# Value products of the attention as one job per step instead of pairs, with a new order of work

## The chip, the cores and the metric

The kernel runs on one core of a Trainium2 chip. The metric is the device time of one launch in microseconds. TensorE (PE in the profile) does the matrix products, VectorE (DVE), ScalarE (ACT) and GpSimd (POOL) work on vectors, and SyncE (SP) issues the DMAs. One program sets every engine's order in advance; engines wait for one another by semaphores only.

## The reference

A transformer block with adaptive normalisation, for 16 batch elements of 1024 tokens and 256 features:

```python
mod = (_silu(c) @ wmod).reshape(16, 6, 1, -1)          # sa, ca, ga, sb, cb, gb
h = _layernorm(x) * (1 + ca) + sa
# attention, 16 heads of 16: scores + ALiBi, causal, softmax, @ V
scores = jnp.einsum('bhqd,bhkd->bhqk', Q, K) / math.sqrt(hd) + slopes * rel
attn = jax.nn.softmax(jnp.where(causal, scores, -jnp.inf), axis=-1)
out = jnp.einsum('bhqk,bhkd->bhqd', attn, V)
x = x + ga * (out @ o_w.T + o_b)
h = _layernorm(x) * (1 + cb) + sb
# feed-forward, 704 wide, activations and weights rounded to an FP4 grid by blocks of 16
x = x + gb * fp4_linear(silu(fp4_linear(h, w_gate)) * fp4_linear(h, w_up), w_down)
```

## The kernel before

**Tiling.** A batch element (below: a batch) is 1024 tokens. Its 16 heads are worked in 4 groups of 4. Attention goes over the scores twice. The maxima half (jobs S, 22 per group, matmuls at L826 and L831) computes scores with the queries on partitions, and VectorE reduces them to a maximum per query (L1251, L1253). The maximum, transposed (MT), is moved into the query tile by a DMA (TOP), so that the attention half can subtract it inside the matmul. The attention half (jobs T, matmuls at L783, L779 and L786) computes scores with the keys on partitions, and ScalarE applies exp and writes the probabilities into the arena in SBUF (L1016).

**Steps.** A group's attention half goes in 12 steps, each one tile of 128 keys against one half (512) of the queries, cut to what is causal: widths 512, 384, 256, 128 for the first half, then 512 five times, 384, 256, 128. That is 4608 columns in all. A step of width 512 or 384 has four T jobs, one per head; the narrow ones have two or one. The arena has `P_SLOTS = 3` slots, each for one step of four heads.

**Value products.** For each step and each of the four heads, TensorE multiplies the values (17 columns: 16 and one of ones, which sums the denominators) by the probabilities (L802). Each float32 product stands as two matmul records in the trace, so a step has eight. The four heads write to output partitions 0, 32, 64 and 96 of one bank, and run in the array side by side. One job PV (L790) handles two steps, s - 1 and s, with s odd: it waits for the exps of step s (`pe.wait_ge(a_free, ...)`), goes through both steps, and adds 1 to the semaphore `pv_done` at the end. All products of one half of the queries add up in one bank; the job that starts a half takes the bank, and a copy on ScalarE (CO, L977) empties it and frees it. ScalarE's exp of a step waits on `pv_done` for the job that holds the step three before it, that is for the whole pair in which this older step stands.

**Other work.** Around the attention stand the layer norm and the projections (TR, U, V: L845, L853, L884), splitting of the queries and keys into three bf16 parts on GpSimd (HIGH, REST, MID, SPL) and the DMAs that lay them out (MOVE), normalising (DEN, RD, RDW, RBC, NUM, MUL), the output projection (O, L904), and the feed-forward half with its rounding to the grid (XR, XQ, HR, HQ on VectorE and GpSimd) and its products (XT L914, GA L925, UP L932, HT L940, DN L947). Batches overlap: the maxima of one batch, the attention of that or the one before and the feed-forward half of the earlier one run at the same time.

**Order.** Nothing sets the order at run time. The class `Plan` builds it once: each job has an engine, a cost, a due time and the jobs that it follows. `settle` (L130) takes, again and again, from all ready jobs the one whose start is earliest, and of equals the one with the earliest due time. The table `SHIFT` adds a constant to the due time for each kind of job and engine; it was found by a search. TensorE's jobs write PSUM through rings that hold at most 4 jobs ahead of ScalarE (A: T, GA, HT, XT, U, V, TR) and 3 ahead of VectorE (D: S, MT, UP, DN, O). PV is in no ring. Two lines price the change of mode between PV and other jobs:

```python
if key[0] == "PE" and MODE.get(key[1][0], 1) != mode:
    t += SWITCH          # 0.095, MODE = {"PV": 4}
```

so in mode 1 a PV that is ready is ranked as if it could start 0.095 us later than any other ready job, and right behind a PV another ready PV is ranked 0.095 us ahead of the rest. Each engine then runs its list strictly in order, with a wait in front of each job: what is queued behind a waiting instruction waits too.

Of the kernel before, what the change touches and what calls it, by code (L numbers as in the profile page):

```python
# [56 lines left out]
TURNS = NS // 2  # L57
# [13 lines left out]
def jobs_of(s):  # L71
    return G // together(s)
# [19 lines left out]
class Plan:  # L92
# [8 lines left out]
    SHIFT = {"ACT CO": 32.0, "ACT GA": -46.0, "ACT HT": -5.0, "ACT KROW": 62.0, "ACT LX": 2.0, "ACT T": -104.0,  # L101
             "ACT TR": 15.0, "ACT U": 55.0, "ACT V": -61.0, "ACT WD": 38.0, "ACT WT": 102.0, "ACT XT": 22.0, "DVE BB": 39.0,
             "DVE BO": -44.0, "DVE DN": -40.0, "DVE HQ": 1.0, "DVE HR": 23.0, "DVE LN": 16.0, "DVE LR": -39.0,
             "DVE MT": 66.0, "DVE N1": 30.0, "DVE N2": 18.0, "DVE N3": 14.0, "DVE O": -15.0, "DVE QROW": -16.0,
# [4 lines left out]
             "POOL MID": -4.0, "POOL MUL": 22.0, "POOL OB": 106.0, "POOL RES": 22.0, "POOL REST": -49.0, "POOL SPL": 61.0,  # L109
# [123 lines left out]
def plan():  # L233
# [64 lines left out]
    def attention(b, at):  # L298
        n, last = 0, ("PE", ("T", b - 1, NG - 1, NS - 1, jobs_of(NS - 1) - 1))
        for g in range(NG):  # L300
            for s in range(NS):
                w = span(s)[1]
                heads = together(s)
                for i in range(jobs_of(s)):
# [5 lines left out]
                       then=(("PE", ("PV", old // (NG * NS), old // NS % NG, old % NS | 1)),) if i == 0 else ())  # L310
# [3 lines left out]
                if s % 2:  # L314
                    first = s - 1 in FIRST
# [124 lines left out]
def adaln_block(nc, x, wq, bq, wk, bk, wv, bv, wo, bo, w_gu, w_down, cond, w_mod, out):  # L440
# [6 lines left out]
    with ExitStack() as ctx:  # L447
# [270 lines left out]
        def _(pe):  # L718
# [47 lines left out]
            def run():  # L766
                for e in PLAN.order["PE"]:
# [22 lines left out]
                    elif kind == "PV":  # L790
                        _, _, g, s = e
                        if s - 1 in FIRST:
                            open_banks(e)
                        if g == 0 and s == 1:
                            pe.wait_ge(a_free, in_a["V", b, 1])
# [679 lines left out]
```

## Time and profile before

| | us |
|---|---|
| median of 3 timed runs | 3579.89 (3577.83 to 3582.98) |
| profiled execution | 3574.78 |
| its span, first to last instruction | 3573.0 |
| TensorE busy | 3351.9 (94%), 21944 matmuls |
| VectorE busy | 3075.8 (86%) |
| ScalarE busy | 1932.1 (54%) |
| GpSimd busy | 1276.6 (36%) |
| value products, L802, busy | 572.5 |

Line numbers (L802) are those of the kernel. Busy time is the union of an engine's instructions. Matmuls are pipelined in the array, so their recorded ends overlap the next start; how much time one takes is read from start to start. "idle before" is time in which the engine had nothing running, and it is put down to the releaser that came last. The mean granted clock of TensorE is 0.980 of full speed; it is below full in the first 250 us and at the very end.

### The profile page before, as it was taken

To read this page: it belongs to the slowest core of one execution; us is meant where nothing else is said; L and a number is where in the kernel's file an instruction comes from. 1 tells how busy PE (TensorE), PEld (TensorE's weight loads), DVE (VectorE), ACT (ScalarE), POOL (GpSimd) and SP (SyncE) were. 2 spreads that over 40 slices of the span, in tenths; PEclk is the share of its full clock that TensorE was granted. 3 is DMA by queue.
4 is the path that set the end of the run, shared out by engine and by line. 5 is a ranking of instruction groups with operands and counts; after the bars stand their busy time and mean duration, and the time that the engine had idled before them with its cause. 6 is when DMAs were issued, how large, how long until landed. Compare 5 with 4: busy or idle time off the path is not lost.

```text
span 3573.0 us, 59366 instructions
## 1 busy us (share of the span) xinstructions
PE 3351.9 (94%) x21944; PEld 2028.7 (57%) x21944; DVE 3075.8 (86%) x5906; ACT 1932.1 (54%) x3630; POOL 1276.6 (36%) x918
## 2 busy tenths in 40 slices
PE   6989999999999999999999999999999999999977
PEld 2335655656656565655655556565565656565556
DVE  8988889888898988889888898988889898887866
ACT  2555555555555555555556555555655555555541
POOL 5122414343243433415343332433324243341333
PEclk7899999999999999999999999999999999999998
DMA  5243333424324342342433333342432433233110
GB/s 119 41 91 46 62 62 48 80 40 76 59 41 77 53 72 43 63 75 42 80 47 62 59 52 67 52 77 40 78 61 41 77 51 69 48 62 57 28 29 12
DMA packets 161812, 208.84 MB, mean 58 GB/s; under 512 B 45172, under 2 KB 101060, under 8 KB 161140
## 3 DMA queue, kind: packets, MB, share of 16 engines
q1 hardware_dynamic: 161524, 205.04, 33.5%
q8 instruction: 176, 2.88, 0.4%
q14 instruction: 112, 0.92, 0.1%
HBM read 66.80 MB, written 18.09 MB: 24 GB/s over the span
## 4 chain that ended last, share of the span: by engine, by line
PE 68%; DVE 21%; ACT 5%; issue 2%; SPq 2%; DMA 2%; POOL 0%; POOLq 0%; DVEq 0%; ACTq 0%
PE banks L802 12%; PE banks L826 11%; PE banks L783 9%; PE banks L947 9%; PE banks L932 7%; PE banks L925 6%; PE banks L853 5%; DVE banks L1253 4%; DVE top L1251 4%; ACT arena L1016 3%; PE banks L884 2%; PE banks L940 2%; PE banks L786 1%; DVE stats L1199 1%; SPq L650 1%
## 5 line engine op out<-in xcount | busy, mean ns | idle before, releaser
L1016 ACT ACTIVATE arena<-banks 128x512 f32<-128x512 f32 (+1 forms) x2432 | 1234.2, 589 | 776.4 <-PE banks L802 316.8
L1253 DVE CUSTOM_DVE_ANT_0 banks<-banks,mask 128x640 f32<-128x640 f32 (+3 forms) x1024 | 1031.5, 1043 | 115.3 <-PE banks L826 108.2
L783 PE MATMUL banks<-qa,ka 105*128 105x512 bf16 (+3 forms) x3072 | 791.6, 329 | 71.9 <-ACT arena L1016 55.0
L826 PE MATMUL banks<-ka,qa 102*128 102x512 bf16 (+3 forms) x3072 | 752.3, 333 | 53.1 <-DVE top L1251 22.6
L802 PE MATMUL banks<-arena,va 128*17 128x512 f32 (+3 forms) x6144 | 572.5, 490 | 11.0 <-DVE top L1253 7.2
L783 PEld LDWEIGHTS banks<-qa,ka 105*128 105x128 bf16 x3072 | 278.3, 97 | 411.1 <-ACT arena L1016 208.8
L826 PEld LDWEIGHTS banks<-ka,qa 102*128 102x128 bf16 x3072 | 262.1, 99 | 400.0 <-issue 96.6
L1150 POOL TENSOR_TENSOR hid<-hid,tm 128x704 f32<-128x704 f32 x128 | 215.0, 1680 | 720.8 <-DVE hid L1227 720.8
L1251 DVE TENSOR_REDUCE top<-banks 128x2 f32<-128x768 f32 (+3 forms) x384 | 386.0, 1040 | 32.9 <-PE banks L831 30.1
L947 PE MATMUL banks<-wdT,hqT 128*128 128x256 f32 x1536 | 363.7, 387 | 3.1 <-ACT hqT L1059 3.0
L947 PEld LDWEIGHTS banks<-wdT,hqT 128*128 128x128 f32 x1536 | 290.3, 193 | 64.5 <-issue 17.3
L802 PEld LDWEIGHTS banks<-arena,va 128*17 128x17 f32 x6144 | 141.3, 97 | 305.5 <-issue 204.8
L786 PE MATMUL banks<-maskT,identb 128*128 128x128 bf16 (+1 forms) x1280 | 296.6, 232 | 0.0
L1054 ACT ACTIVATE hid<-banks 128x352 f32<-128x352 f32 x256 | 114.3, 465 | 247.8 <-PE banks L925 247.3
L1150 POOL TENSOR_TENSOR xb<-xb,tm 128x512 f32<-128x512 f32 x64 | 82.4, 1287 | 372.1 <-DVE xb L1227 372.1
L1167 POOL TENSOR_TENSOR xr<-xr,delta 128x256 f32<-128x256 f32 x128 | 102.3, 799 | 291.3 <-DVE delta L1373 290.9
L1365 DVE TENSOR_TENSOR hid<-hid,banks 128x704 f32<-128x704 f32 x128 | 113.1, 884 | 95.3 <-PE banks L932 95.2
L1153 POOL TENSOR_TENSOR hid<-hid,scaleH 128x704 f32<-128x704 f32 x128 | 178.7, 1396 | 10.0
L925 PE MATMUL banks<-wguTh,xqTh 128*128 128x352 f32 x512 | 180.8, 353 | 1.5 <-DVE xqTl L1316 1.5
L1116 POOL TENSOR_SCALAR parts<-xa 128x1024 bf16<-128x1024 f32 x64 | 73.6, 1150 | 290.8 <-ACT xa L1030 142.9
L925 PE MATMUL banks<-wguTl,xqTh 128*128 128x352 f32 x512 | 166.2, 325 | 0.0
L925 PE MATMUL banks<-wguTh,xqTl 128*128 128x352 f32 x512 | 166.2, 325 | 0.0
(163 smaller groups left out, 5687.1 us busy)
## 6 DMA issues: line engine op xcount, KB each, us to landing
qa<-parts SPq DMA_DIRECT2D x384, 128.0 KB
ka<-parts SPq DMA_DIRECT2D x384, 128.0 KB, 6.6
xa<-in_x SPq DMA_DIRECT2D x16, 1024.0 KB, 8.6
xr<-in_x SPq DMA_DIRECT2D x64, 256.0 KB, 2.7
out_x<-xr SPq DMA_DIRECT2D x64, 256.0 KB, 3.9
rsumT<-rsum_dram SPq DMA_DIRECT2D x63, 256.0 KB
onT<-oT SPq DMA_DIRECT2D x252, 64.0 KB, 5.7
ffn_rows<-rows_dram SPq DMA_DIRECT2D x16, 256.0 KB, 3.1
```

Source lines behind the costliest of these rows:

```text
L783: mm = pe.matmul(ps[:, m * w:(m + 1) * w], ks[0:KT, h, kt * P:(kt + 1) * P], qs[0:KT, h, q0:q0 + w], start=heads < G and m == 0, stop=head ...
L786: mm = pe.matmul(ps[:, 0:heads * w].rearrange("p (h q) -> p h q", h=heads)[:, :, 0:P], identb[:, :], maskT[:, :].unsqueeze(1).broadcast_to ...
L802: mm = pe.matmul(out[32 * h:32 * h + VW, :], va[:, kt, g * G + h, :], probs[:, step % P_SLOTS, h, 0:w], start=step in FIRST, stop=step in ...
L826: mm = pe.matmul(ps[:, at:at + z - a], qs[0:KS, h0 + m, qt * P:(qt + 1) * P], ks[0:KS, h0 + m, a:z], start=qt > 0 and m % paired == 0, sto ...
L925: mm = pe.matmul(ps[:, 0:FH], x, w[:, e[3] * FH:(e[3] + 1) * FH], start=(n == 0), stop=(n == len(terms) - 1))
L932: mm = pe.matmul(ps[:, k * BANK:k * BANK + FH], x, w[:, FF + k * FH:FF + (k + 1) * FH], start=(n == 0), stop=(n == len(terms) - 1))
L947: mm = pe.matmul(ps[:, 0:D], hqT[t % 2][:, c, :], wdT[:, c, :], start=(c == 0), stop=(c == FC - 1))
L1016: nc.scalar.activation(probs[:, s % P_SLOTS, j * heads:(j + 1) * heads, 0:w], ps[:, 0:heads * w].rearrange("p (h q) -> p h q", h=heads), A ...
L1150: nc.gpsimd.tensor_tensor(u, u, m, ALU.subtract).then_inc(gridded, 1)
L1153: nc.gpsimd.tensor_tensor(blocks, blocks, sc.unsqueeze(2).broadcast_to((P, w // BLOCK, BLOCK)), ALU.mult).then_inc(quant_done, 1)
L1251: nc.vector.tensor_reduce(tops, ps, AX.X, ALU.max).then_inc(d_free, 1)
L1253: nc.vector.tensor_tensor_reduce(out=ps, in0=ps, in1=mask[:, S - w:S], scale=1.0, scalar=MASKED, op0=ALU.add, op1=ALU.max, accum_out=tops) ...
```

## The change

One job PV now handles one step. There are 12 per group in place of 6, each waits for its own step's exps alone, and adds 1 to `pv_done`, whose counts at the waiting places are adapted. The exp that reuses a slot waits for one older step, no longer for a pair. The bank of a half is opened by the half's first step. The planner sees PV as single jobs of 1.69 ns per column + 0.02 us, each after the one before it. Where its order puts two or three of them next to each other, they form one run. All values of `SHIFT` are new, so every engine's order is another. The products themselves are the same.

```diff
-    SHIFT = {"ACT CO": 32.0, "ACT GA": -46.0, "ACT HT": -5.0, ... "ACT T": -104.0,
+    SHIFT = {"ACT CO": 94.0, "ACT GA": -28.0, "ACT HT": -22.0, ... "ACT T": 8.0,
...
-             ... "PE PV": -84.0, "PE S": 6.0, "PE T": 2.0, ...
+             ... "PE PV": 2.0, "PE TR": 33.0, ...
@@ attention
-                       then=(("PE", ("PV", old // (NG * NS), old // NS % NG, old % NS | 1)),) if i == 0 else ())
+                       then=(("PE", ("PV", old // (NG * NS), old // NS % NG, old % NS)),) if i == 0 else ())
...
-                if s % 2:
-                    first = s - 1 in FIRST
-                    p.add("PE", ("PV", b, g, s), 1.69e-3 * (w + span(s - 1)[1]) + 0.02, due + 3, ("ACT", ("T", b, g, s, jobs_of(s) - 1)),
-                          ("PE", ("PV", b, g, s - 2)) if s > 1 else None, ("ACT", ("V", b, 1)) if (g, s) == (0, 1) else None, lag=0.22,
-                          banks=1 if first else 0, holder=("ACT", ("CO", b, g, c)) if first else None)
+                p.add("PE", ("PV", b, g, s), 1.69e-3 * w + 0.02, due + 3, ("ACT", ("T", b, g, s, jobs_of(s) - 1)),
+                      ("PE", ("PV", b, g, s - 1)) if s else None, ("ACT", ("V", b, 1)) if (g, s) == (0, 0) else None, lag=0.22,
+                      banks=1 if s in FIRST else 0, holder=("ACT", ("CO", b, g, c)) if s in FIRST else None)
@@ TensorE, kind PV
-                        if s - 1 in FIRST:
+                        kt, c = STEPS[s]
+                        q0, w = span(s)
+                        if s in FIRST:
                             open_banks(e)
...
-                        for step in (s - 1, s):
-                            ...
-                            for h in range(G):
-                                mm = pe.matmul(out[32 * h:32 * h + VW, :], va[:, kt, g * G + h, :],
-                                               probs[:, step % P_SLOTS, h, 0:w], start=step in FIRST,
-                                               stop=step in LAST, skip_group_check=True)
+                        for h in range(G):
+                            mm = pe.matmul(out[32 * h:32 * h + VW, :], va[:, kt, g * G + h, :],
+                                           probs[:, s % P_SLOTS, h, 0:w], start=s in FIRST,
+                                           stop=s in LAST, skip_group_check=True)
                         mm.then_inc(pv_done, 1)
@@ ScalarE
-                        act.wait_ge(pv_done, n * TURNS + (LAST[c] + 1) // 2)
+                        act.wait_ge(pv_done, n * NS + LAST[c] + 1)
...
-                        old = (b * NG + g) * NS + s - P_SLOTS
-                        if j == 0 and old >= 0:
-                            act.wait_ge(pv_done, old // 2 + 1)
+                        if j == 0 and (b * NG + g) * NS + s >= P_SLOTS:
+                            act.wait_ge(pv_done, (b * NG + g) * NS + (s - P_SLOTS + 1))
```

## Rows read from the trace of the kernel before

**Rows 1.** The page: busy shares, and the chain that ended last by engine.
```profile
PE 3351.9 (94%) x21944; PEld 2028.7 (57%) x21944; DVE 3075.8 (86%) x5906; ACT 1932.1 (54%) x3630; POOL 1276.6 (36%) x918
...
PE 68%; DVE 21%; ACT 5%; issue 2%; SPq 2%; DMA 2%; POOL 0%; POOLq 0%; DVEq 0%; ACTq 0%
```
**Rows 2.** Busy time by stretch: start:end, length, each engine's us (count), clock, DMA, GB/s.
```profile
0.00:250.00 250.00, 199.46 (x1046) 83.20 (x1046) 218.83 (x490) 107.76 (x184) 77.89 (x57) 0.84 0.43 82
250.00:3350.00 3100.00, 2982.53 (x19920) 1815.01 (x19920) 2708.71 (x5154) 1745.70 (x3296) 1119.80 (x801) 1.00 0.35 59
3350.00:3573.00 223.00, 169.96 (x982) 130.46 (x979) 148.24 (x264) 78.59 (x152) 78.92 (x61) 0.87 0.08 22
1450.00:1662.60 212.60, 205.22 (x1370) 125.47 (x1369) 187.38 (x356) 119.88 (x226) 78.60 (x57) 1.00 0.36 60
1662.60:1875.20 212.60, 205.22 (x1370) 125.20 (x1368) 186.90 (x356) 119.70 (x226) 78.43 (x57) 1.00 0.34 59
```
**Rows 3.** Waits of TensorE, 250 to 3350 us: who <- whom: us, times, longest.
```profile
PE banks L783 <- ACT arena L1016: 46.5, 70, 1.0
PE banks L826 <- DVE top L1251: 20.3, 44, 0.9
PE banks L826 <- DVE top L1253: 16.2, 20, 1.4
...
PE banks L802 <- ACT arena L1016: 1.4, 1, 1.4
```
**Rows 4.** Waits of TensorE in the last 223 us.
```profile
PE banks L940 <- POOL hid L1153: 21.2, 6, 8.4
```
**Rows 5.** Waits of ScalarE, 250 to 3350 us.
```profile
ACT arena L1016 <- PE banks L802: 292.6, 132, 7.6
```
**Rows 6.** The page's groups: line engine op, shapes, count | busy, mean ns | idle before.
```profile
L802 PE MATMUL banks<-arena,va 128*17 128x512 f32 (+3 forms) x6144 | 572.5, 490 | 11.0 <-DVE top L1253 7.2
```
**Rows 7.** TensorE in order of time: start, length, engine line op, count. Runs and a step.
```profile
1508.99 0.38 PE L783 MATMUL banks<-qa,ka 105*128 105x512 bf16 x1
1509.30 1.70 PE L802 MATMUL banks<-arena,va 128*17 128x512 f32 x16
...
1511.85 0.84 PE L802 MATMUL banks<-arena,va 128*17 128x256 f32 x16
1512.63 0.44 PE L940 MATMUL banks<-ident,hid 128*128 128x128 f32 x2
...
1516.75 0.38 PE L783 MATMUL banks<-qa,ka 105*128 105x512 bf16 x1
1516.97 0.60 PE L826 MATMUL banks<-ka,qa 102*128 102x512 bf16 x2
...
1520.98 1.91 PE L802 MATMUL banks<-arena,va 128*17 128x512 f32 x16
1522.82 0.26 PE L838 MATMUL banks<-identb,top_parts 128*96 128x128 bf16 x1
```
**Rows 8.** ScalarE, then TensorE, in order of time around 1605 us.
```profile
1602.47 3.58 ACT L1016 ACTIVATE arena<-banks 128x512 f32<-128x512 f32 x8
1607.38 1.09 ACT L1016 ACTIVATE arena<-banks 128x512 f32<-128x512 f32 x2 [1.33 <-PE banks L802]
...
1605.62 1.70 PE L802 MATMUL banks<-arena,va 128*17 128x512 f32 x16
1607.25 0.55 PE L826 MATMUL banks<-ka,qa 102*128 102x512 bf16 x2
```
**Rows 9.** ScalarE from 1524 us, then all engines around 1538 us.
```profile
1523.99 3.54 ACT L1016 ACTIVATE arena<-banks 128x512 f32<-128x512 f32 x7 [0.44 <-PE banks L783]
...
1538.53 2.62 ACT L1016 ACTIVATE arena<-banks 128x384 f32<-128x384 f32 x6
...
1539.08 0.34 PE L783 MATMUL banks<-qa,ka 105*128 105x384 bf16 x1 [0.92 <-ACT arena L1016]
...
1540.77 1.70 PE L802 MATMUL banks<-arena,va 128*17 128x512 f32 x16
```

More of the change, by code:

```diff
@@ L56 @@
 FIRST, LAST = (0, T // 2), (T // 2 - 1, NS - 1)
-TURNS = NS // 2
 DIAGONAL = [s for s, (kt, c) in enumerate(STEPS) if c == kt // (T // 2)]
@@ L99 @@
     APART = ("LN", "XR", "XQ", "HR", "HQ", "N2", "N3", "LR", "SM", "WQ", "QROW")
[L101 to L104, printed above, removed]
[4 rows of a table removed]
-             "POOL MID": -4.0, "POOL MUL": 22.0, "POOL OB": 106.0, "POOL RES": 22.0, "POOL REST": -49.0, "POOL SPL": 61.0,
[3 rows of a table removed]
+    SHIFT = {"ACT CO": 94.0, "ACT GA": -28.0, "ACT HT": -22.0, "ACT KROW": -36.0, "ACT LX": -8.0, "ACT T": 8.0,
+             "ACT TR": 17.0, "ACT U": 3.0, "ACT V": 6.0, "ACT WD": -13.0, "ACT WT": 49.0, "ACT XT": 104.0, "DVE BB": -32.0,
+             "DVE BO": -25.0, "DVE DN": -93.0, "DVE HQ": -21.0, "DVE HR": -21.0, "DVE LN": 6.0, "DVE LR": 47.0,
+             "DVE MT": -18.0, "DVE N1": 15.0, "DVE N2": 14.0, "DVE N3": 11.0, "DVE O": -52.0, "DVE QROW": -17.0,
[4 rows of a table added]
+             "POOL MID": -40.0, "POOL MUL": -37.0, "POOL OB": -76.0, "POOL RES": -45.0, "POOL REST": 23.0,
+             "POOL SPL": -12.0, "POOL WG": -23.0, "POOL XQ": -24.0, "SP DEN": -36.0, "SP DOWN": -13.0, "SP FGATE": 61.0,
+             "SP FROW": -56.0, "SP GROW": -28.0, "SP MOVE": 27.0, "SP NUM": 53.0, "SP OUT": -72.0, "SP RBC": 12.0,
+             "SP RDW": 70.0, "SP SROW": -66.0, "SP TOP": 16.0, "SP XA": -10.0, "SP XIN": 23.0}
     PATIENCE = {"ACT": 0.8, "POOL": 0.3, "SP": 0.2}
@@ L791, in run @@
                         _, _, g, s = e
-                        if s - 1 in FIRST:
+                        kt, c = STEPS[s]
+                        q0, w = span(s)
+                        if s in FIRST:
                             open_banks(e)
-                        if g == 0 and s == 1:
+                        out = bank(("PV", b, g, FIRST[c]))[:, q0 - c * BANK:q0 - c * BANK + w]
+                        if g == 0 and s == 0:
                             pe.wait_ge(a_free, in_a["V", b, 1])
                         pe.wait_ge(a_free, in_a["T", b, g, s, jobs_of(s) - 1])
-                        for step in (s - 1, s):
-                            kt, c = STEPS[step]
-                            q0, w = span(step)
-                            out = bank(("PV", b, g, FIRST[c] + 1))[:, q0 - c * BANK:q0 - c * BANK + w]
-                            for h in range(G):
-                                mm = pe.matmul(out[32 * h:32 * h + VW, :], va[:, kt, g * G + h, :],
-                                               probs[:, step % P_SLOTS, h, 0:w], start=step in FIRST,
-                                               stop=step in LAST, skip_group_check=True)
+                        for h in range(G):
+                            mm = pe.matmul(out[32 * h:32 * h + VW, :], va[:, kt, g * G + h, :],
+                                           probs[:, s % P_SLOTS, h, 0:w], start=s in FIRST,
+                                           stop=s in LAST, skip_group_check=True)
                         mm.then_inc(pv_done, 1)
@@ L976, in run @@
                             act.wait_ge(sums_in, 16 * n)
-                        nc.scalar.copy(oT[:, c * BANK:(c + 1) * BANK], bank(("PV", b, g, FIRST[c] + 1))).then_inc(o_free, 1)
+                        nc.scalar.copy(oT[:, c * BANK:(c + 1) * BANK], bank(("PV", b, g, FIRST[c]))).then_inc(o_free, 1)
                         continue
@@ L1001, in run @@
                         if b:
-                            act.wait_ge(pv_done, b * NG * TURNS)
+                            act.wait_ge(pv_done, b * NG * NS)
                         act.wait_ge(a_full, full)
```

11 rows, old and new, of the table SHIFT are left out of this document.

## The prediction, made before the changed kernel ran

> **What bounds the kernel now.** I read the page first: TensorE is busy 94% of a 3573.0 us span, and 68% of the chain that ended last is its work [rows 1]. Then the stretches: between 250 and 3350 us it is busy 2982.5 of 3100 us (96.2%) at the full granted clock, while VectorE is busy 2708.7 (87%) and ScalarE 1745.7 (56%) [rows 2]. Two stretches of 212.6 us, one batch each, have the same TensorE time to the hundredth and the same number of matmuls, so the middle of the kernel is one pattern repeated, and a change of 1 us in it is worth about 15 us in all [rows 2]. What is left to win without removing TensorE work is its idle time: in the middle 118 us, 7.4 us per batch. The table of waits names who ends it: 46.5 us (70 waits) are score jobs of the attention half (L783) waiting for an exp on ScalarE to give back a ring place, and 36.5 us (64 waits) are score jobs of the maxima half (L826) waiting for a VectorE reduction [rows 3]. The start and the end hold another 50 and 53 us, mostly on setup and on GpSimd's requantising in the last batch [rows 2, 4].
>
> The pair rule has a visible cost on ScalarE: it waits 292.6 us in 132 waits for value products (L802), its largest wait [rows 5]. An exp that reuses an arena slot needs a whole pair done. ScalarE isn't the bound, so this costs nothing by itself; it counts only where it stops L783 afterwards.
>
> **The price of a run of value products.** The edit doesn't change the products: 12 steps per group, 64 groups, 768 steps, as before. It changes how many separate runs they form. Now there are 384, 24 per batch (6144 matmul records in the line's group, 16 in each run) [rows 6, 7]. Each run is entered from and left to another use of the array. From the order in time [rows 7]: a run of 512+512 columns takes 1.84 us from its first matmul to the next engine job (1520.98 to 1522.82), one of 256+128 columns 0.78 us (1511.85 to 1512.63). The difference, 1.06 us for 640 columns, is 1.66 ns a column; 1024 columns are then 1.70 us, and 0.14 us is left for leaving the run. Entering: the L783 matmul at 1508.99 streams for 0.22 us (1516.75 to 1516.97 is such a step), but the run begins 0.31 us after it, so 0.09 us more. A run costs 0.23 us over its columns. A check: L802 is busy 572.5 us [rows 6], its 64 x 4608 columns at 1.66 ns are 490 us, and the rest, 82.5 us over 384 runs, is 0.21 us each, so 0.21 to 0.23.
>
> This is where a rule of the Trainium skill speaks against the change: the page TensorEngine Tiling (Array Packing), section Tiling Modes, says that changing the tiling mode drains TensorE, while moving between tiles of a mode doesn't. The trace agrees as far as it goes (0.14 and 0.09 us around a run, and nothing visible between the two steps inside one). By that rule alone, with every step apart, the change would be a plain loss; that is a rival below.
>
> **Part 1, single jobs.** Bounds: with every step apart there are 768 runs, 384 more x 0.23 = +88 us. With three steps together wherever three arena slots allow, 256 runs, 128 fewer = -29 us. What decides is whether the next step is already exponentiated when the product of the last one ends, because the planner adds its switch price to every candidate that needs another mode. Both occur in this trace. At 1602.47 ScalarE does eight exps up to 1606.05, through a third step, while the pair that started at 1605.62 runs to 1607.25: three steps could stand together there, and ScalarE then waited 1.33 us for that pair [rows 8]. At the other end, exps of one step end at 1527.53, and its partner is only ready after the exps that begin at 1538.53: those two would be 10 us apart [rows 9]. In the batch of rows 2 I laid the end of each exp group beside the start of each run: in 14 of 24 pairs the following step's exps were over before the pair ended (a third could join), and in 10 of 24 TensorE had an idle spell while the first step of the pair lay ready (a split would be invited; six different spells of these are over 0.25 us long). I take 3 more runs per batch net: all 10 splits, and 7 joins, half of the 14. 16 x 3 x 0.23 = +11 us. Ends for the range: -4 per batch (-15 us) and +12 per batch (+44 us).
>
> **Part 2, idle time that a single product fills or prevents.** The clear case is the 0.92 us before 1539.08, in which L783 waits for ScalarE, whose table load and exps come late, and the step whose exps ended at 1527.53 lies ready all the time [rows 9]. The pair rule forbids it. A single of 512 columns costs 0.85 + 0.23 us and would cover that gap whole. The same spell comes back with every batch, and so do ones of about 0.9, 0.8, 0.4, 0.4 and 0.3 us: 3.7 us per batch in six spells. Each filled one returns at most its length (the run's price is in part 1). Some gaps have the wrong work next to them, since VectorE, which is 87% busy, sets when the L826 ring frees; filling a spell doesn't move its end. I take 2.3 us per batch, 60% of the six. Over 15 batches that is -35 us. Ends: 0 (the spells are filled by work that then is missing later), and -65 us, over half of all the 118 us [rows 2].
>
> **Part 3, looser waits and new ones.** An exp now waits for one older step, not for that step's pair. Every ScalarE wait of rows 5 for L802 gets shorter or goes; ScalarE is 56% busy, so the gain is only through L783 and is inside part 2. New waits: TensorE waits for the exps before each product, 768 times for 384. Queued behind such a wait are the score jobs of both halves and all feed-forward matmuls, in order, and both VectorE and ScalarE behind those. Now only 1.4 us of TensorE idle in the middle comes from a value product waiting for its exps [rows 3]; the plan places it late enough. Twice that is 3 us; I take 1, and 0 to 10 as ends if the new order puts them tighter. The bank of each output half is opened by the first step alone, some 2 to 5 us earlier; L802 waits 7.2 us for VectorE, the bank kind of wait [rows 6], which I leave as it is, -3 to +7. The additional semaphore increments have no row; at one per run they are within the 0.14 us already priced.
>
> **Part 4, the new order.** All engines' sequences move, queues of GpSimd and SyncE included. The trace of before can't show that. The parts of it that could matter are the start (50 us of TensorE idle) and the last batch (53 us; 21.2 us of it in L940 waiting for GpSimd's requantised rows) [rows 2, 4]. I take 0 with -15 and +15 us as ends: nearly a third of the larger one.
>
> **Sum.** +11 - 35 + 1 + 0 = -23 us on the span: 3573.0 to 3550. The profiled execution took 3574.78 us, 1.8 more than its span, and the median of the timed runs is 3579.89, 5.1 above that; so the time is 3550 + 6.9 = 3557 us, 0.64% less than before. A difference under 0.2% (7 us) can't be told from no change by these measurements.
>
> **The rivals.**
> (a) The steps stay apart. With VectorE and ScalarE giving ring places back in small bits, the planner finds TensorE free early and places each product as soon as its exps are over. Half of the pairs split: 12 more runs per batch, 192 in all, +44 us; gaps filled give back 20 of it. Time 3580 + 24 = 3604 us, slower. It decides from the point where added runs x 0.23 us exceeds the idle time that goes: with 35 us from part 2 that is 150 added runs, 10 per batch. For it: pairs start close behind their exps already (the runs at 1540.77 and 1605.62 begin before ScalarE has ended the chain of exps that made them ready, at 1541.15 and 1606.05 [rows 8, 9]). Against it: TensorE is 96% busy, so work is nearly always waiting, and the product is what can be put off.
> (b) Nothing to win: the idle spells are set by VectorE's rhythm and come back elsewhere, and runs stay near 24 per batch. 3580 us, within 0.2%. For it: VectorE has 21% of the chain [rows 1] and 87% busy.
> (c) The freedom is used fully: products in threes where the trace shows a third ready, 4 fewer runs per batch (-15 us), and 60 of the 118 us idle gone. 3580 - 75 = 3505 us. Against it: three together means that all three slots are full and ScalarE stands still during it.
> (d) The change of order does something else: the middle is as (b), the last batch or the start moves by up to 15 us either way. It is spread over the other cases.
>
> **How the numbers follow.** Forecast case 0.42, from 3535 to 3585 us, centre 3557; (a) 0.28, 3578 to 3640, centre 3604; (b) 0.14, 3571 to 3589; (c) 0.16, 3480 to 3535. Faster by over 0.2% (below 3573): 0.34 of the forecast case and all of (c), 0.50. Slower (above 3587): 0.25 of (a), 0.03 of (b) and (d), 0.28. The rest, 0.22, is within. The range leaves out the upper quarter of (a) and the lower half of (c): 3512 to 3615. The forecast case's own range is 3535 to 3585.
>
> **What would show it.** Number of runs of L802: 384 now; right near 430, (a) at 550 or more, (c) at 320 or less. TensorE busy over the span: 3352 now, about 3363 if right (more busy and yet shorter), 3385 or more in (a). TensorE idle in the middle: 118 us now, about 83 if right. The row L783 waiting for ScalarE falls from 46.5 to under 25, and ScalarE's wait for L802 from 292.6 to under 150. L826 waiting for VectorE stays at about 36 us. The prediction is wrong if these idle rows stand as they are, if runs are over 530, or if the end of the kernel, not its middle, moves.

## The result

| | before | after |
|---|---|---|
| median of the timed runs, us | 3578.86 (4 runs) | 3498.55 (3496.23 to 3499.77, 4 runs) |
| ratio to before | | 0.9773 (0.9756 to 0.979) |
| span of the profiled execution, us | 3573.0 | 3494.4 |
| TensorE busy, us | 3351.9 | 3326.2 |
| TensorE idle (span less busy), us | 221.1 | 168.2 |
| runs of value products | 383 | 394 |

The change makes the kernel 80 us (2.3%) faster. The sign was forecast, the size was not: 23 us were forecast, and 3498.55 lies below the range. There are 383 runs before, not 384, because two of the 384 jobs stand side by side. In the kernel after, L780 and L783 are what L783 and L786 were, L798 what L802 was, L822 what L826 was, L1011 the exp, L1246 and L1248 the reductions.

The page of after, the same parts as [rows 1, 6]:

```profile
span 3494.4 us, 59380 instructions
...
PE 3326.2 (95%) x21944; PEld 2028.7 (58%) x21944; DVE 3026.8 (87%) x5906; ACT 1948.9 (56%) x3628; POOL 1258.4 (36%) x918
...
PE 69%; DVE 21%; ACT 4%; issue 2%; DMA 2%; SPq 1%; POOL 1%; DVEq 0%; POOLq 0%; ACTq 0%
...
L1011 ACT ACTIVATE arena<-banks 128x512 f32<-128x512 f32 (+1 forms) x2432 | 1248.2, 582 | 770.2 <-PE banks L780 402.7
...
L780 PE MATMUL banks<-qa,ka 105*128 105x512 bf16 (+3 forms) x3072 | 774.3, 328 | 33.0 <-ACT arena L1011 21.5
L822 PE MATMUL banks<-ka,qa 102*128 102x512 bf16 (+3 forms) x3072 | 744.7, 332 | 33.7 <-DVE top L1246 12.0
L798 PE MATMUL banks<-arena,va 128*17 128x512 f32 (+3 forms) x6144 | 572.5, 489 | 10.4 <-ACT arena L1011 8.0
```

The work is the same, 21944 matmuls, and L798 is busy 572.5 us as before. L780 is busy 17.3 us less (791.6 before) and L822 7.6 us less (752.3).

Busy time of after by stretch, columns as in [rows 2] (TensorE first); the last row is one batch:

```profile
0.00:250.00 250.00, 203.22 (x1114) 85.45 (x1115) 224.84 (x506) 115.03 (x198) 82.11 (x60) 0.87 0.46 88
250.00:3270.00 3020.00, 2943.36 (x19772) 1808.07 (x19771) 2647.07 (x5128) 1751.64 (x3269) 1098.18 (x798) 1.00 0.36 60
3270.00:3494.40 224.40, 179.60 (x1062) 135.21 (x1060) 154.94 (x274) 82.23 (x163) 78.09 (x60) 0.88 0.08 21
1450.00:1658.90 208.90, 204.28 (x1375) 126.11 (x1376) 183.83 (x357) 121.24 (x227) 76.86 (x57) 1.00 0.36 61
```

TensorE idle in the middle is 76.6 us of 3020 (117.5 of 3100 before); in the first 250 us 46.8 us (50.5); in the last 224 us 44.8 us (53.0). A batch takes 208.9 us for 212.6.

Waits of TensorE in the middle, as [rows 3], and of ScalarE, as [rows 5]:

```profile
PE banks L780 <- ACT arena L1011: 16.7, 34, 1.0
PE banks L822 <- DVE top L1246: 8.4, 27, 0.9
PE banks L798 <- ACT arena L1011: 7.4, 29, 0.3
PE banks L822 <- DVE hid L1360: 7.0, 12, 0.9
PE banks L822 <- DVE top L1248: 6.5, 10, 1.1
```

```profile
ACT arena L1011 <- PE banks L798: 156.9, 99, 6.1
```

The score jobs of the attention half wait 16.7 us in 34 waits (46.5 in 70 before), those of the maxima half 21.9 us over the three VectorE rows (36.5 over the two of before, [rows 3]). ScalarE's wait for value products has nearly halved, from 292.6 us.

The form of the runs was not what I had thought possible. Read from the order in time over the whole span, 188 of the 394 runs hold one step, 85 two, 74 three and 47 four. One of the fours, on TensorE, and what ScalarE does:

```profile
1532.14 2.35 PE L798 MATMUL banks<-arena,va 128*17 128x512 f32 x32
1534.42 0.60 PE L780 MATMUL banks<-qa,ka 105*128 105x512 bf16 x2
```

```profile
1533.26 4.18 ACT L1011 ACTIVATE arena<-banks 128x512 f32<-128x512 f32 x8 [5.37 <-PE banks L798]
```

32 matmul records are four steps. The arena has three slots, so the fourth step's exp can't begin before the first of the four products is done (1532.14 plus some 0.85 us). It begins at 1533.26, is one exp of 128 columns for all four heads, and is over while the run goes on. By the planned order all 47 fours end in such a step or in one of 256 columns: 33 are steps 0 to 3, 13 are steps 7 to 10, one is steps 8 to 11. ScalarE stood idle 5.37 us before that exp; it is busy 56% and has room for this.

By batch, counted in the planned order, there are 24 runs in each of the 14 batches between the first and the last, as before; the first and the last have 29 each. In most of these batches 11 of the 24 pairs are split, and 11 times a product directly follows one that in before belonged to another run.

### The profile page after: what moved, and what is told of

The parts are those of the page before. It is cut to its first block, busy times and chain, and to the rows that moved or that the text cites. A ratio compares the mean times of both kernels' runs of the same rounds, so it can differ in the third digit from the quotient of the medians.

```text
span 3494.4 us, 59380 instructions
## 1 busy us (share of the span) xinstructions
PE 3326.2 (95%) x21944; PEld 2028.7 (58%) x21944; DVE 3026.8 (87%) x5906; ACT 1948.9 (56%) x3628; POOL 1258.4 (36%) x918
## 4 chain that ended last, share of the span: by engine, by line
PE 69%; DVE 21%; ACT 4%; issue 2%; DMA 2%; SPq 1%; POOL 1%; DVEq 0%; POOLq 0%; ACTq 0%
PE banks L798 11%; PE banks L822 11%; PE banks L780 10%; PE banks L943 9%; PE banks L921 6%; PE banks L928 6%; PE banks L849 5%; DVE top L1246 3%; PE banks L880 3%; DVE banks L1248 3%; ACT arena L1011 3%; PE banks L936 2%; PE banks L783 2%; DVE stats L1194 2%; DMA sums<-oT 1%
## 5 line engine op out<-in xcount | busy, mean ns | idle before, releaser
L1011 ACT ACTIVATE arena<-banks 128x512 f32<-128x512 f32 (+1 forms) x2432 | 1248.2, 582 | 770.2 <-PE banks L780 402.7
L1248 DVE CUSTOM_DVE_ANT_0 banks<-banks,mask 128x640 f32<-128x640 f32 (+3 forms) x1024 | 1032.1, 1046 | 194.5 <-PE banks L822 188.7
L780 PE MATMUL banks<-qa,ka 105*128 105x512 bf16 (+3 forms) x3072 | 774.3, 328 | 33.0 <-ACT arena L1011 21.5
L822 PE MATMUL banks<-ka,qa 102*128 102x512 bf16 (+3 forms) x3072 | 744.7, 332 | 33.7 <-DVE top L1246 12.0
L798 PE MATMUL banks<-arena,va 128*17 128x512 f32 (+3 forms) x6144 | 572.5, 489 | 10.4 <-ACT arena L1011 8.0
L822 PEld LDWEIGHTS banks<-ka,qa 102*128 102x128 bf16 x3072 | 254.2, 99 | 390.8 <-DVE top L1248 76.8
L780 PEld LDWEIGHTS banks<-qa,ka 105*128 105x128 bf16 x3072 | 274.5, 97 | 341.0 <-ACT arena L1011 118.4
L1246 DVE TENSOR_REDUCE top<-banks 128x2 f32<-128x768 f32 (+3 forms) x384 | 386.4, 1039 | 11.2 <-PE banks L827 10.2
L798 PEld LDWEIGHTS banks<-arena,va 128*17 128x17 f32 x6144 | 139.5, 96 | 298.2 <-issue 167.2
L783 PE MATMUL banks<-maskT,identb 128*128 128x128 bf16 (+1 forms) x1280 | 295.5, 231 | 0.0
L1162 POOL TENSOR_TENSOR xr<-xr,delta 128x256 f32<-128x256 f32 x128 | 94.6, 739 | 266.1 <-DVE delta L1368 266.1
L1136 POOL TENSOR_TENSOR xr<-xr,ga_row 128x512 f32<-128x512 f32 x64 | 81.9, 1280 | 258.6 <-DMA xr<-in_x 245.1
L1054 ACT COPY hqT<-banks 128x512 f32<-128x512 f32 (+1 forms) x256 | 110.1, 484 | 102.4 <-PE banks L936 101.2
```

What stands on the lines that cost most here:

```text
L780: mm = pe.matmul(ps[:, m * w:(m + 1) * w], ks[0:KT, h, kt * P:(kt + 1) * P], qs[0:KT, h, q0:q0 + w], start=heads < G and m == 0, stop=head ...
L783: mm = pe.matmul(ps[:, 0:heads * w].rearrange("p (h q) -> p h q", h=heads)[:, :, 0:P], identb[:, :], maskT[:, :].unsqueeze(1).broadcast_to ...
L798: mm = pe.matmul(out[32 * h:32 * h + VW, :], va[:, kt, g * G + h, :], probs[:, s % P_SLOTS, h, 0:w], start=s in FIRST, stop=s in LAST, ski ...
L822: mm = pe.matmul(ps[:, at:at + z - a], qs[0:KS, h0 + m, qt * P:(qt + 1) * P], ks[0:KS, h0 + m, a:z], start=qt > 0 and m % paired == 0, sto ...
L1011: nc.scalar.activation(probs[:, s % P_SLOTS, j * heads:(j + 1) * heads, 0:w], ps[:, 0:heads * w].rearrange("p (h q) -> p h q", h=heads), A ...
L1246: nc.vector.tensor_reduce(tops, ps, AX.X, ALU.max).then_inc(d_free, 1)
```

## Where in the kernel the time went

The first product of a batch can be found by counting 384 records of the line (48 steps of eight) per batch. The first products of the third and of the last batch, in before, in after and in one of the experiments (5, both edits: the new order with most steps put back beside their partners and with exps that wait for the pair):

```profile
502.34 1.05 PE L802 MATMUL banks<-arena,va 128*17 128x512 f32 x8
...
3266.28 1.05 PE L802 MATMUL banks<-arena,va 128*17 128x512 f32 x8
```

```profile
486.61 1.05 PE L798 MATMUL banks<-arena,va 128*17 128x512 f32 x8
...
3200.19 1.05 PE L798 MATMUL banks<-arena,va 128*17 128x512 f32 x8 [0.49 <-DVE top L1248]
```

```profile
500.45 1.05 PE L822 MATMUL banks<-arena,va 128*17 128x512 f32 x8
...
3262.91 1.05 PE L822 MATMUL banks<-arena,va 128*17 128x512 f32 x8 [0.49 <-DVE top L1273]
```

```profile
span 3558.3 us, 59380 instructions
```

The 13 batches between take 2763.9 us in before, 2713.6 in after and 2762.5 in the experiment. So the middle gives 50.4 us, 3.9 us per batch; the stretch up to the third batch 15.7 us (502.34 to 486.61), and the last one 12.5 us (306.7 to 294.2). The three make up the 78.6 us between the spans. With that experiment's products, the middle is as slow as before to 1.5 us and the beginning to 1.9 us; only the last stretch keeps its gain (3558.3 - 3262.9 = 295.4 us, 11.3 less than before). So this order gives no gain in the middle without the single jobs. What it gives by itself is the end.

The first and the last stretch hold batches too (two and one). At 3.9 us per batch, 7.9 of the 15.7 us and 8.6 of the 12.5 us lie beyond the rate of the middle. Part of the 7.9 may be TensorE's clock: between 180 and 250 us the granted clock was 0.90 in before and 1.00 in after. But it was 1.00 in the experiment as well, which gained only 1.9 us there.

TensorE's own time in the middle, at the full granted clock in both (before, then after, columns as in [rows 2]):

```profile
502.34:3266.28 2763.94, 2666.67 (x17786) 1629.87 (x17785) 2422.61 (x4581) 1557.90 (x2938) 1020.59 (x729) 1.00 0.35 59
```

```profile
486.61:3200.19 2713.58, 2648.29 (x17784) 1631.65 (x17783) 2376.49 (x4580) 1575.16 (x2938) 1002.71 (x729) 1.00 0.36 61
```

Of the 50.4 us, 32.0 are idle time (97.3 to 65.3) and 18.4 are busy time (2666.7 to 2648.3), though the matmuls (to two at the edges) and the number of runs are the same.

## The experiments

Each was timed beside the kernel before on the same chip; differences are those between the two medians, and one to the kernel after is taken through the kernel before.

**1. What a run costs.** A matmul of one column with zero weights, over the full width of the array, into the same bank; once between the two steps of each pair, once behind them:

```diff
                         for step in (s - 1, s):
...
+                            if step == s:
+                                pe.matmul(bank(("PV", b, g, FIRST[c] + 1))[:, 0:1], mask[:, 0:P], identb[:, 0:1],
+                                          start=False, stop=False, skip_group_check=True)
```

> The kernel before with one matmul of one column, full width of the array and zeros as weights, put between the two steps of each of the 384 pairs, into their own bank: every run is cut in two without moving any other job. If a run costs 0.23 us and TensorE sets the end: 384 x 0.23 = +88 us and up to 0.1 us each for the added matmul itself, so +88 to +125 us. If the cost of a run is mostly hidden by waits that are there anyway: +20 to +60 us.

> The kernel before with the same added matmul of one column and zeros, now behind the second step of each of the 384 pairs, where the run is left anyway: as many added matmuls as in the run that put it between the steps (3644 us), but no added entering and leaving. If the 66 us there are the price of runs: within 15 us of before here, 3575 to 3594 us. If they are the price of the added matmul: 3620 us or more.

Between: 3644.35 us, +65.8 (ratio 1.0185, 1.0166 to 1.0203). Behind: 3585.97 us, +7.0 (1.002, 1.001 to 1.0029). The busy shares of both, and one split run of the first:

```profile
PE 3438.8 (94%) x22328; PEld 2027.2 (56%) x22328; DVE 3060.9 (84%) x5906; ACT 1931.9 (53%) x3630; POOL 1273.0 (35%) x918
```

```profile
PE 3367.4 (94%) x22328; PEld 2038.7 (57%) x22328; DVE 3070.6 (86%) x5906; ACT 1931.0 (54%) x3630; POOL 1276.0 (36%) x918
```

```profile
1503.81 1.05 PE L805 MATMUL banks<-arena,va 128*17 128x512 f32 x8
1504.80 0.18 PE L802 MATMUL banks<-identb,mask 128*128 128x1 bf16 x1
1504.91 1.05 PE L805 MATMUL banks<-arena,va 128*17 128x512 f32 x8
1505.89 0.26 PE L841 MATMUL banks<-identb,top_parts 128*96 128x128 bf16 x1
```

TensorE is busy 86.9 us more than before, 0.226 us for each of 384 added visits (the matmul of one column included; behind the pair it adds 15.5 us in all, 0.04 each); from a first product to the next engine job it is now 2.08 us (1503.81 to 1505.89), where the same widths took 1.84 [rows 7]. But the end comes only 65.8 us later, 0.17 us each, or 0.15 with what the added matmul costs by itself taken off. The price of 0.21 to 0.23 us was right as TensorE time; the rest was covered by waits, for TensorE's idle time fell from 221.1 to 204.1 us. The first result lies below the range I had expected for a price paid in full (+88 to +125), for that reason, and just above the one for a mostly hidden price (+20 to +60).

A run differs from its neighbours in two things, the four column groups and, beside the bf16 scores, the number format. The trace of before tells them apart. Read from start to start between 500 and 3200 us, less the columns, where TensorE has no idle time listed, entering a run costs 0.096 us and leaving it 0.115 to 0.118 us, 0.21 us together; it is the same whether the neighbour is a float32 job (37 runs entered from L940) or a bf16 one. Between float32 and bf16 jobs outside the runs the middle value is 0.002 us (673 places). So the price goes with the change to the column groups and back, not with the format.

**2. The early release alone.** The order of before and its pairs, with `pv_done` counted at each step:

```diff
-                        mm.then_inc(pv_done, 1)
+                            mm.then_inc(pv_done, 1)
...
-                            act.wait_ge(pv_done, old // 2 + 1)
+                            act.wait_ge(pv_done, old + 1)
```

> The kernel before with its order and its 384 pair runs untouched; only the semaphore counts each step of a pair as it ends, so that an exp waits for the one step whose slot it takes. Theory A (the gain comes from the looser wait of the exps, which lets score jobs of the attention half, L783, run on): 10 to 25 us faster than before, L783 waiting for ScalarE falls from 55 to under 40 us, ScalarE waiting for L802 from 317 to under 250 us. Theory B (the gain is the newly searched order and the freedom to place steps apart, the release alone is worth nothing in an order laid out without it): within 7 us of before.

3571.18 us, -7.4 (0.9978, 0.9968 to 0.9989). ScalarE's wait for L802 fell from 316.8 to 226.0 us:

```profile
ACT arena L1016 <- PE banks L802: 226.0, 142, 7.1
```

The score jobs' wait for ScalarE did not fall with it (56.1 us, 55.0 before). The order of before was laid out with the pair's wait in it; that little is queued where the earlier release would help is my reading, not shown. Less than A's 10 to 25; B's 7 us lies within the interval (some 4 to 11 us), so in this order the release is worth little.

**3. Single products in the old order's idle spells.** The kernel of experiment 2, with products as single jobs, and 36 first steps moved up TensorE's list in front of a score job that had waited for ScalarE while they were ready; all else as before:

```diff
+PLAN.order["PE"] = [o for e in PLAN.order["PE"] for o in ([("PV", e[1], e[2], e[3] - 1), e] if e[0] == "PV" else [e])]
+EARLIER = {(0, 0, 6): (0, 0, 8, 0), (0, 1, 6): (0, 1, 7, 2), ...}
+for (_b, _g, _s), _t in EARLIER.items():
+    _o = PLAN.order["PE"]
+    _o.remove(("PV", _b, _g, _s))
+    _o.insert(_o.index(("T", *_t)), ("PV", _b, _g, _s))
```

> The kernel before's order, products as single jobs with a release for each step, and 36 first steps of pairs moved up TensorE's list in front of a score job that waited for ScalarE in the trace of the same order (28.4 us of such spells in all); runs 383 to 419. By the prediction's part 2 each filled spell returns most of its length: -28 + 36 x 0.2 = about 20 us faster than the order with early release (3571), 3545 to 3560 us. If the spells come back later: 3571 to 3580 us.

3549.6 us, -28.0 (0.9923, 0.9908 to 0.9937), that is 20.6 us beyond the early release. Score jobs waiting for ScalarE, over the whole span, with early release and with the filled spells:

```profile
PE banks L783 <- ACT arena L1016: 56.1, 85, 2.0
```

```profile
PE banks L798 <- ACT arena L1030: 40.9, 67, 1.5
```

That a ready product moved in front of a waiting score job shortens the kernel, as part 2 had it, is shown, at nearly three quarters of the listed length (28.4 us of spells), with the price of 36 more runs already paid. Two things besides the filled spell are not told apart from it here: a product taken early also frees its slot earlier (ScalarE's wait for products goes from 226.0 to 200.6 us), and every first step, moved or not, now waits for its own exps alone.

**4. The new order with its steps put back together.** 150 of the 178 even steps that stand apart from their partner are moved down TensorE's list to just before it:

```diff
+LATER = {(0, 0, 0), (0, 0, 4), ...}
+for _b, _g, _s in sorted(LATER):
+    _o = PLAN.order["PE"]
+    _o.remove(("PV", _b, _g, _s))
+    _o.insert(_o.index(("PV", _b, _g, _s + 1)), ("PV", _b, _g, _s))
```

> The kernel after with every engine's order as it is, but 150 of its 178 separated steps with even number are moved down TensorE's list to stand right in front of their partner (the other 28 would leave the engines waiting for one another for ever). Runs fall from 394 to 293. If the place of the single products is worth nothing in itself: 101 runs x 0.17 to 0.23 us = 17 to 23 us faster, 3476 to 3482 us. If taking a product early, so that its slot is free for the exp three steps on, is what this order lives on: slower than after by 20 us or more.

3521.96 us, 0.9846 (0.9831 to 0.9861): 55.7 us ahead of before, where after is 80.3 ahead, so it costs 24.6 us, though there are 293 runs for 394. It isn't quite the pair form: of the 293 runs 173 hold two steps, 55 three and 64 four. The 101 fewer runs alone would have given some 15 us by the price of experiment 1. By this estimate the early place is worth about 40 us in this order.

**5. The new order with exps that wait for the pair.** At 355 of 383 places; at the other 28 the engines would wait for one another for ever. Then both edits at once:

```diff
-                            act.wait_ge(pv_done, (b * NG + g) * NS + (s - P_SLOTS + 1))
+                            old = (b * NG + g) * NS + s - P_SLOTS
+                            act.wait_ge(pv_done, (old if (b, g, s) in STEPWISE else old | 1) + 1)
```

> The kernel after, but the exp that reuses a slot waits for both steps of the old pair, at 355 of 383 places (at the other 28 the engines would wait for one another for ever). Products and every order as in after. If the looser wait is a large part of the open 50 us: 20 to 60 us slower than after, 3520 to 3560 us, and score jobs of the attention half wait 60 us or more for ScalarE, against 21.5. If it is worth what it was in the old order: 5 to 12 us slower, 3504 to 3511 us.

> Both at once: 150 separated steps put back in front of their partners (3522 us by itself) and the wait for the pair at 355 places. This is nearly the pair form in the new order of all other work. If the form is what counts: 3550 us or more, most of the 80 us gone. If the new order of the other work counts: 3520 to 3535 us, some 50 us still ahead of before.

The release alone: 3520.26 us, 0.9837 (0.9821 to 0.9854), 21.2 us lost. Both: 3559.24 us, 0.9943 (0.9929 to 0.9958), 60.1 us lost, more than the two by themselves (45.8). In the 13 middle batches experiment 4 takes 2732.7 us, the release alone 2733.7 and both 2762.5, against 2713.6 in after. TensorE's waits for exps over the whole span, in after (score jobs of the attention half, products, score jobs of the maxima half), then with the pair's release (products first), then with both (maxima half, products, attention half):

```profile
PE banks L780 <- ACT arena L1011: 21.5, 45, 1.4
...
PE banks L798 <- ACT arena L1011: 8.0, 31, 0.4
...
PE banks L822 <- ACT arena L1011: 3.0, 4, 0.9
```

```profile
PE banks L801 <- ACT arena L1015: 26.8, 95, 0.9
PE banks L783 <- ACT arena L1015: 21.2, 44, 1.5
```

```profile
PE banks L846 <- ACT arena L1036: 26.8, 57, 1.0
PE banks L822 <- ACT arena L1036: 26.0, 92, 0.9
PE banks L804 <- ACT arena L1036: 25.6, 63, 1.4
```

The release that cost 7 us to lack in the old order costs 21 in the new one. I had expected the loss to show as score jobs waiting 60 us or more; that was wrong, they stay at 21.2 us. What grows is the products' own wait for exps, 8.0 to 26.8 us, since the exps may now start later, and with both edits the maxima half waits for banks that unread scores hold, 3.0 to 26.8 us. Meanwhile ScalarE waits longer for products (164.1 us over the whole span in after):

```profile
ACT arena L1015 <- PE banks L801: 271.8, 155, 6.7
```

**6. Tables of due times crossed over.** Single jobs with the old table, pairs with the new one:

> The kernel after (single jobs) with the table of due times of the kernel before, so the planner lays a new order with the old table. Its order has 428 runs of value products against 384 and 394. Theory A (freedom of single jobs brings the gain, whatever the table): at least half of the 80 us, 3500 to 3540 us, in spite of 44 more runs (+10 us). Theory B (the search brings it): no better than before, 3575 to 3630 us.

> The kernel before (pairs) with the table of due times of the kernel after. 384 runs. Theory A (single jobs bring the gain): 3570 us or more. Theory B (the new table brings it and doesn't care for pairs): 3500 to 3540 us. A table searched for single jobs may fit pairs badly, then over 3640 us, which would say only that table and form belong together.

3644.95 us (1.0185, 1.0167 to 1.0202) and 3750.87 us (1.0481, 1.0458 to 1.0504). Both are slower than either kernel. Theory A of the first expectation falls all the same: freedom with whatever table brings no gain. For the rest, it is what the last sentence of the second expectation allowed for: a table belongs to its form, and crossing them doesn't tell which of the two brought the gain. Experiments 3 to 5 tell more, because they leave all other orders alone. But 4 and 5 undo the form in an order laid out for single jobs, so they show what this order loses without the form, not what the form would bring in any order.

**7. Searches of equal effort.** Some 3000 tries on the planner's own length, from the same old table, for pairs and for single jobs; and the same from the new table:

> The kernel before, pairs kept, with its table of due times improved by a further search of some 3000 tries on the planner's own length (a second search from the old table, one of two of equal effort). Theory A (single jobs bring the gain, a search alone finds little for pairs): within 15 us of before, 3560 to 3580 us. Theory B (the search brings it): 3500 to 3540 us.

> Single jobs, started from the same old table, with the same search of some 3000 tries. With the old table itself this form took 3645 us, 66 us more than before. Theory A (single jobs give a better order once the table fits them): at least 60 us below the 3645, and below the pairs of equal search by 15 us or more. Theory B (the form doesn't matter): equal to the pairs of equal search within 10 us.

> The kernel after, with its table searched further by some 3000 tries; the planner's own length falls by 11 us. If the chip follows the planner's length: 3480 to 3492 us, faster than both. If the table of the kernel after is fitted to the chip by other means than this length: 3500 to 3530 us.

Pairs 3557.87 us (0.9942, 0.9925 to 0.9958); single jobs 3639.04 us (1.0165, 1.015 to 1.018); the kernel after further 3500.05 us (0.9781, 0.9766 to 0.9795), the same as after. The planner's length is a poor judge: for the single jobs it had fallen by 72 us and the chip's time by 6; for pairs by 9 and the chip gave 21, with the middle at 212.5 us a batch as before, so at the ends alone. The pairs came out 2 us below theory A's range. The single jobs missed both theories: with equal search they are 81 us slower than the pairs, and 60 slower than before. So single jobs without an order that suits them bring nothing. Whether pairs with a luckier or longer search would come nearer to the kernel after is not shown. The runs do say that 21 us are to be had for pairs from order alone, and where: the first product of the third batch starts 4.8 us earlier (497.56 us), the last stretch is 11.9 us shorter (294.8), and the 13 batches between take 2762.8 us, 1.1 less than before.

**8. The function tables.** The long wait in [rows 9] follows a table load of 1.28 us on ScalarE:

```profile
1537.23 1.28 ACT L1016 ACT_TABLE_LOAD   x1 [1.74 <-PE banks L786]
```

The gate passed without SiLU (this leaves out part of the computation), in before and in after:

```diff
-                                             ps[:, 0:FH], ACT.Silu).then_inc(a_free, 1)
+                                             ps[:, 0:FH], ACT.Identity).then_inc(a_free, 1)
```

> The kernel before with the SiLU of the feed-forward gate left out (the gate passes unchanged), so that ScalarE has no function tables to change between exp and SiLU, some 120 loads of 1.28 us less. In the trace of before, waits of score jobs of the attention half of over 0.15 us with a table load shortly before them add up to 44 us, against 17 us in after. If those loads cause them: 30 to 50 us faster than before, 3530 to 3550 us. If the waits come from ScalarE's order and not from the loads: within 10 us.

> The kernel after with the same part left out. If the new order hides the table loads better: only 5 to 20 us faster than after, 3478 to 3494 us, so that the gap between the two forms shrinks from 80 to 50 or 60 us. If the loads matter equally in both: the gap stays at 80 us.

3557.78 us (0.9951, 0.9934 to 0.9967), -19.9, and 3483.28 us (0.9737, 0.9723 to 0.9752), 14.0 below after. The first lies between the two expectations (30 to 50, or within 10). The gap between the forms is 74.5 us for 80.3. That the new order hides the loads better falls as a main cause; the difference of 6 us is no larger than the noise of such a comparison.

**9. The rule again, on the new order.** 28 more products moved up in front of score jobs that waited over 0.25 us in the trace of after (25.3 us of spells), the edit as in experiment 3:

> The kernel after with 28 single products moved up TensorE's list in front of a score job that waited over 0.25 us in its trace while the product's exps were over (25.3 us of such spells); runs 394 to 419. By the rate of the old order (28.4 us of spells gave 21.6 us): 15 to 22 us faster than after, 3477 to 3484 us, faster than both kernels. If the new order has no such slack: 3495 to 3510 us.

3484.91 us, 0.9737 (0.9722 to 0.9751), 94.5 us ahead of before and 14.2 ahead of after, a little short of the 15 I had expected at least. It is the fastest kernel of this study that does the whole computation, with 419 runs for 394:

```profile
PE 3332.1 (96%) x21944; PEld 2024.6 (58%) x21944; DVE 3022.6 (87%) x5906; ACT 1947.8 (56%) x3628; POOL 1258.3 (36%) x918
```

TensorE is now busy 95.7% of 3482.6 us.

## Why the prediction was right in kind and wrong in size

**The price of a run, right.** 0.21 to 0.23 us as TensorE time; 0.226 measured with a matmul of one column in it, 0.21 read from the edges of the runs. The Trainium skill tells of a drain at a change of tiling mode (TensorEngine Tiling (Array Packing), Tiling Modes). The trace agrees so far as a price is paid at both edges of a run, 0.096 and 0.12 us, whatever the neighbour's number format. That the change would be a plain loss by it (rival a) did not come about, because the order holds 394 runs, not 550 or more.

**Part 1, mis-sized upwards.** I took 3 more runs per batch, +11 us, from 10 splits and 7 joins. There are 11 more in all, some +2.5 us by my price, and none in the batches between the first and the last: 11 splits, as good as forecast, and 11 joins. I had ruled out more than three together for want of slots, and 47 runs hold four. Case (c) leaned on the same error.

**Part 2, the step that failed.** Experiments 3 and 9 show that a product moved in front of a wait pays, as this part had it. The size was taken from TensorE's listed idle time: 2.3 us per batch, all told -35 us. Idle time in the middle fell by just that kind of amount, 7.5 to 5.0 us per batch (97.3 and 65.3 us over 13 batches). The prediction's 7.4 is that of one batch; its 118 us over the whole middle are 8.1 per batch. But busy time per batch fell too, from 205.1 to 203.7 us, where I had it rise by 0.7, and over the whole span from 3351.9 to 3326.2 us, where I had forecast about 3363. I took busy time as fixed work. So of the 55.6 us that the span is shorter than forecast, 37 lie in busy time (25.7 less in place of 11 more) and 19 in idle time (52.9 less in place of 34).

A matmul's record runs on after the next could start (0.38 us recorded, 0.22 us to the next start, the L783 step of [rows 7]), so a wait behind it is counted as busy for its first 0.16 us, and a shorter wait isn't listed at all. Take the 13 middle batches, where the clock was full in both kernels, and read from start to start the time from a matmul of the attention half to the next one, where that is of the attention or the maxima half, less the columns streamed at full clock. It adds up to 123.6 us before and 85.0 after, 38.6 less. The idle time listed in front of the same matmuls fell by 13.2 us only (55.9 to 42.7), so 25.4 us of waits went that no list shows. They lie at the places where the next start came over 0.04 us late, after a wait for an exp or a reduction: what is hidden there falls from 51.2 to 25.5 us. These 25.4 us are more than the 18.4 by which busy time fell; some went back at other places.

The Trainium skill says in Perfetto Trace Analysis, Identifying the Most-Contended Engine, that matmul busy share is no good measure of how close a kernel is to its limit, because the instructions are pipelined. The trace agrees, with 25.7 us of "busy" gone over the span and not one matmul fewer. Read from start to start, the slack of the old order was larger than its list of waits, and case (c) should have had more weight.

**Part 3, half right.** I put the looser wait inside part 2, at nothing of its own. In the old order it is worth 7.4 us, and in the new one 21. Without it and without the place of the products the new order loses 60 of its 80 us. The wait of ScalarE for products fell nearly as far as said (156.9 us in the middle, under 150 forecast). Products waiting for exps rose from 1.4 to 7.4 us, 6 us more where I took 1; 0 to 10 were the ends. That L826 would keep its waits for VectorE was wrong: 36.5 to 21.9 us.

**Part 4, out of sight.** 0 was taken with 15 us either way. Start and end gave 28.2 us, some 16.5 of them beyond the middle's rate for their three batches, so just outside these ends. The last stretch gave 12.5 us, of which 11.3 stay with the pairs put back, and the pairs of experiment 7 gain 11.9 there from order alone, so it is the order. The beginning gave 15.7 us, of which only 1.9 stay, so most of it needs the form.

**The rivals.** (a), fell: 394 runs. (b) was right that the runs stay near 24 per batch, but fell: the idle spells did not come back. (c) had about the right size (3505 us forecast, 3498.55 measured), but on a false ground: not 4 fewer runs per batch, but as many as before, and more time won from waits than the list of waits shows. That was luck. Its chance was 0.16.

**What stays open.** Some 20 us of the 80 stay in the new order when the form is undone (3579.41 to 3559.24); the trace puts 11.3 us of them in the last stretch, and the cause inside it was not tried. The other 60 are what this order loses without the form. They are not the form's share by itself: experiment 7 has single jobs in another order that are slower than pairs, and in the order of before filled spells and the release together gave 28 us. How much of the 60 needs both, form and order, is not shown. In the experiment nearest to pairs 28 steps and 28 waits could not be put back, and many runs were longer than a pair. Why both edits together cost more than their sum was not tried.

## What to carry to other kernels

Where one engine sets the pace, a job that can be put off (its inputs ready, nobody waiting soon) is best kept small and used to fill the spells in which that engine's next job waits; look for them in the order in time, and move the ready job in front of the waiting one. Price the slack of a pipelined engine from start to start, not by its idle time, since short waits hide in the recorded ends. When a form and a searched order change together, crossing the two tells little. Undo the form inside the new order, see which stretch gives its time back, and read the result as what that order needs, not as the form's share.

## What was new about the hardware

Going into the array's use in four column groups costs 0.096 us of TensorE time and going out of it 0.12 us, with float32 and with bf16 neighbours alike, while a change between the two formats alone costs 0.002 us (experiment 1). An added visit makes TensorE 0.226 us busier (86.9 us over 384, with a matmul of one column in it), but the end only 0.15 to 0.17 us later on an engine that is busy 94%. The rest had been waits.
